# A two-layer attention and FFN kernel: attention sums from one pass of products, the output projection moved behind the second down product

## The reference

```python
x = x + autocorrelation(layernorm(x), ctx, ctx)      # FFT correlation, 8 best lags, weighted shifts
x = x + linear_with_8_adapters(layernorm(x))
x = x + grouped_attention(layernorm(x), ctx, ctx)    # 32 query heads, 8 key/value heads of 16
x = x + ffn(layernorm(x))                            # below
```

```python
h = relu(hidden @ up_w) ** 2
shared = h @ down_w
moe = (hidden @ fc1_w @ expert_w) * sum(top_2(hidden @ gate_w))
return layernorm(shared + moe @ fc2_w) * gamma + beta
```

## Time and profile before

| what | value |
|---|---|
| median of 3 runs | 685.81 us (684.9 to 689.61) |
| the profiled execution | 687.42 us |
| its span | 685.6 us |
| TensorE, share of the span | 95% |
| VectorE, ScalarE, GpSimd | 75%, 63%, 55% |
| granted clock of TensorE | 0.999 |

### The profile page before, as it was taken

How to read it: one execution, slowest core, us unless ns; L and a number is a source line. 1 busy time by engine, 2 the same in 40 slices (tenths; PEclk the granted TensorE clock), 3 DMA queues, 4 the chain that set the end, 5 groups by cost and what they waited for, 6 DMA issues and landing times.

```text
span 685.6 us, 12653 instructions
## 1 busy us (share of the span) xinstructions
PE 654.6 (95%) x3964; PEld 482.3 (70%) x3964; DVE 511.4 (75%) x1140; ACT 432.0 (63%) x793; POOL 378.5 (55%) x464
## 2 busy tenths in 40 slices
PE   7889999999999898999999999999999999998986
PEld 3455666666656476788778787887878878786775
DVE  4999998999975877777677677776777767775444
ACT  4788888888746785574655846658367474674221
POOL 1388999888775534435455354554454545535351
PEclk9999999999999999999999999999999999999999
DMA  8334434352126321121212312113021221211000
GB/s 269 121 109 124 139 123 124 123 180 98 62 94 173 117 79 33 46 64 61 63 35 57 90 33 61 45 49 90 31 61 54 69 61 31 61 31 47 17 16 31
DMA packets 32551, 54.37 MB, mean 79 GB/s; under 512 B 5344, under 2 KB 7136, under 8 KB 32512
## 3 DMA queue, kind: packets, MB, share of 16 engines
q1 hardware_dynamic: 32512, 53.90, 26.6%
HBM read 36.84 MB, written 8.39 MB: 66 GB/s over the span
## 4 chain that ended last, share of the span: by engine, by line
PE 78%; DVE 11%; issue 4%; DMA 3%; ACT 3%; POOL 1%; SPq 0%; POOLq 0%; DVEq 0%; ACTq 0%
PE ps_b L1295 8%; PE ps_b L1297 7%; PE ps_b L1296 7%; PE wide L1295 7%; PE wide L1297 6%; PE wide L1296 6%; PE ps_b L1496 4%; PE ps_a L1340 4%; PE bank L1432 3%; DMA ctx_t<-in_ctx 3%; PE wide L1422 3%; PE ps_b L1350 3%; PE ps_a L1295 2%; PE ps_a L1297 2%; PE wide L1550 2%
## 5 line engine op out<-in xcount | busy, mean ns | idle before, releaser
L780 POOL TENSOR_TENSOR va<-mv,small 128x1 f32<-128x1 f32 x80 | 15.3, 192 | 149.0 <-DVE mv L1274 79.5
L745 ACT ACTIVATE stage<-wide 128x512 f32<-128x512 f32 x30 | 16.3, 595 | 83.8 <-PE bank L1597 83.7
L868 POOL TENSOR_TENSOR y_l<-y,y_h 128x512 fp32r<-128x512 f32 x16 | 21.9, 1370 | 72.5 <-ACT y_h L653 72.5
L1142 DVE RECIPROCAL y<-ps_b 128x256 f32<-128x256 f32 x32 | 55.9, 1748 | 0.4 <-PE ps_b L1496 0.4
L676 ACT ACTIVATE probs<-wide 128x1024 f32<-128x1024 f32 x32 | 32.8, 1025 | 36.1 <-PE wide L1550 36.1
L1295 PE MATMUL wide<-up_h,t_h 128*128 128x512 f32 x128 | 52.1, 407 | 1.5 <-DVE t_l L1226 1.5
L1297 PE MATMUL wide<-up_h,t_l 128*128 128x512 f32 x128 | 50.9, 398 | 0.0
L1296 PE MATMUL wide<-up_l,t_h 128*128 128x512 f32 x128 | 50.4, 394 | 0.0
L1295 PE MATMUL ps_b<-down_h,ht_h 128*128 128x512 f32 x120 | 49.6, 413 | 0.4 <-DVE ht_l L1214 0.4
L782 POOL TENSOR_TENSOR rs<-va,small 128x1 f32<-128x1 f32 x80 | 44.5, 557 | 6.3
L1297 PE MATMUL ps_b<-down_h,ht_l 128*128 128x512 f32 x120 | 47.2, 393 | 0.0
(11 more groups left out here) (244 smaller groups left out, 2155.9 us busy)
## 6 DMA issues: line engine op xcount, KB each, us to landing
q_stack<-qt_h SPq DMA_DIRECT2D x128, 64.0 KB, 2.0
ctx_t<-in_ctx SPq DMA_DIRECT2D x16, 256.0 KB, 2.7
x_res<-in_x SPq DMA_DIRECT2D x16, 256.0 KB, 2.9
x_in<-x_rows SPq DMA_DIRECT2D x16, 256.0 KB, 2.7
ctx_t<-in_ctx_turned SPq DMA_DIRECT2D x16, 256.0 KB, 2.9
x_res<-x_rows SPq DMA_DIRECT2D x16, 256.0 KB, 2.9
out<-stage SPq DMA_DIRECT2D x15, 256.0 KB, 3.0
x_in<-in_x SPq DMA_DIRECT2D x8, 256.0 KB, 3.0
```

What stands on the lines that cost most here:

```text
L1142: dve.reciprocal(y[:, :, b, :], part[:, 1]).then_inc(S["den_s"], 1)
```

## The change

`attend` keeps its form for the tiles 0 and 1 (`apart(t)`). For the others `vbd` holds ones beside the values (set once, at tile 2), and a product takes 64 rows, one head of one batch, so that the numerators and the denominators of head h come out of one product, into bank 2 + h, on neighbouring groups of 16 partitions. ScalarE copies both banks into `sums` and writes the first head's numerators, masked by `place[0]`, into y (`attended_out`). Eight moves bring the denominators onto the numerators' partitions (`denominators`, 16 partitions of 2 KB each). VectorE adds the second head's numerators (`numerators`), takes the reciprocal in two instructions (`inverted`: 128 and 384 elements) and multiplies (`attended`).

The output projection goes behind `down(i, 1)`, its products with `y_l` come last, and the maxima's transposes stand ahead of these. `turned_hidden` and the down products come earlier; keys, queries and scores change places. On the other engines the calls follow. In the opening turn `down_low(0)` moves behind the reciprocals, `down_low(1)` into turn 0, and `down_high(1)` to the turn's end. The increments of `vf_s` and `dft_lo`, for which no engine waited, are dropped.

```diff
+            def denominators(t):
+                if live(t) and not apart(t):
+                    wait(sp, S["wo_ps"], t)
+                    for h in range(2):
+                        sp.wait_ge(S["sums_s"], 3 * (t - APART) + h + 1)
+                        for p in range(PAIRS):
+                            at, beside = STACK * p + HD * h, STACK * p + HD * (1 - h)
+                            sp.dma_start(den[at:at + HD], sums[h][beside:beside + HD]).then_inc(S["den_in"], 16)
...
             def body2(i):
                 load2(i + 4)
-                stacked(i + 3)
                 residual(i + 2)
+                denominators(i + 2)
                 t = i - 1
                 if live(t):
                     sp.wait_ge(S["o_s"], t + 1)
                     sp.dma_start(rows(out_rows, t), z_of(t)).then_inc(S["out_stored"], 16)
+                stacked(i + 3)
```

```diff
                 if opening(i):
-                    guard_rows(2)
-                    query_high(3)
-                    down_high(1)
+                    y_high(i + 2)
+                    queries_stacked(i + 3)
                 else:
-                    query_high(i + 4)
-                    guard_rows(i + 3)
+                    queries_stacked(i + 3)
+                    y_high(i + 2)
+                guard_rows(i + 3)
+                query_high(i + 4)
                 weights_of(i + 3, 0)
+                weights_of(i + 3, 1)
                 t = i + 1
                 if live(t):
                     act.wait_ge(S["rt_out_ps"], 2 * t + 2)
...
+                if opening(i):
+                    down_high(1)
                 if closing(i):
                     hidden_high(NT - 1, 1)
-                weights_of(i + 3, 1)
```

```diff
+            def attended_out(t):
+                if live(t) and not apart(t):
+                    act.wait_ge(S["pv_ps"], 2 * t + 2)
+                    act.wait_ge(S["qy_ps"], capped(1, t + 2))
+                    for h in range(2):
+                        act.activation(sums[h][:].rearrange("p g b q -> p b g q"),
+                                       bank[2 + h].rearrange("p (b g q) -> p b g q", b=2, g=GROUPS), ACT.Copy
+                                       ).then_inc(S["sums_s"], 1)
+                    wait(act, S["wo_ps"], t)
+                    act.activation(y[:].rearrange("p g b q -> p b g q"),
+                                   bank[2].rearrange("p (b g q) -> p b g q", b=2, g=GROUPS), ACT.Copy, scale=place[0]
+                                   ).then_inc(S["sums_s"], 1)
```

VectorE, functions and turn:

```diff
+                elif live(t):
+                    dve.wait_ge(S["sums_s"], 3 * (t - APART) + 3)
+                    dve.scalar_tensor_tensor(y[:], sums[1][:], place[1], y[:], ALU.mult, ALU.add).then_inc(S["den_s"], 1)
+
+            def inverted(t, groups):
+                if live(t) and not apart(t):
+                    dve.wait_ge(S["den_in"], DEN_MOVES * (t - APART + 1))
+                    dve.reciprocal(den[:, groups], den[:, groups]).then_inc(S["den_s"], 1)
+
+            def attended(t):
+                if live(t) and not apart(t):
+                    dve.wait_ge(S["den_s"], 2 * APART + 3 * (t - APART + 1))
+                    dve.tensor_tensor(y[:], y[:], den[:], ALU.mult).then_inc(S["y_s"], 1)
...
                 t = i
                 if live(t) and not final(t):
                     hidden_low(t, 0)
+                keys_low(i + 3)
+                queries_low(i + 3)
+                numerators(i + 2)
+                if isinstance(i, int) and i == 0:
+                    down_low(1)
+                context_low(i + 4)
+                maxima(i + 3, 0)
+                inverted(i + 2, slice(0, 1))
+                t = i
+                if live(t) and not final(t):
+                    hidden_low(t, 1)
+                inverted(i + 2, slice(1, GROUPS))
                 attended(i + 2)
+                maxima(i + 3, 1)
+                normalised(i + 4)
...
+                if opening(i):
+                    down_low(0)
                 values(i + 3)
+                third(i + 2)
+                norm_low(i + 4)
...
+                keys_biased(i + 4)
+                third_norm(i + 2)
                 queries(i + 4)
```

Between `normalised` and `down_low(0)` stand the maximum and the sum of the gate; between `norm_low` and `keys_biased` the sum z and its statistics. GpSimd does the square of the hidden rows ahead of `y_low`, and `y_low` follows it. TensorE:

```diff
+            def attend_ready(t):
                 if live(t):
                     pe.wait_ge(S["vbd_s"], t + 1)
                     wait(pe, S["kv_s"], capped(1, t + 2))
                     wait(pe, S["z_s"], t - 2)
+                    pe.wait_ge(S["probs_s"], 2 * t + 2)
...
+                elif live(t):
+                    for b in range(2):
+                        for p in range(PAIRS):
+                            for h in range(2):
+                                k = slice(SEQ * h, SEQ * (h + 1))
+                                last = pe.matmul(bank[2 + h][STACK * p:STACK * (p + 1), HALF * b:HALF * (b + 1)],
+                                                 vbd[k, b, p].rearrange("k h d -> k (h d)"), probs[k, b, p, :],
+                                                 start=True, stop=True)
                         last.then_inc(S["pv_ps"], 1)
...
+            def output(t, between):
+                if live(t):
+                    pe.wait_ge(S["y_hi"], t + 1)
+                    for g in range(GROUPS):
+                        pe.matmul(bank[2], cols(y_h, g, P), cols(wo_h, g, D), start=(g == 0), stop=False)
+                        pe.matmul(bank[2], cols(y_h, g, P), cols(wo_l, g, D), start=False, stop=False)
+                    between()
                     pe.wait_ge(S["y_lo"], t + 1)
                     for g in range(GROUPS):
+                        last = pe.matmul(bank[2], cols(y_l, g, P), cols(wo_h, g, D), start=False, stop=(g == GROUPS - 1))
                     last.then_inc(S["wo_ps"], 1)
```

More of the change, by code:

```diff
@@ L94, in constants @@
     small[:, ONES0:ONES0 + 2 * HD] = np.kron(np.eye(2), np.ones((SEQ, HD)))
+    small[:, PLACE0:PLACE0 + 2] = np.tile(np.repeat(np.eye(2), HD, axis=0), (PAIRS, 1))
     for p in range(PAIRS):
@@ L136, in build @@
         ones_bd = small[:, ONES0 - FIRST:ONES0 - FIRST + 2 * HD]
+        place = [small[:, PLACE0 - FIRST + h:PLACE0 - FIRST + h + 1] for h in range(2)]
         half, eps, minus = (small[:, c - FIRST:c - FIRST + 1] for c in (HALF0, EPS0, MINUS0))
@@ L157, in build @@
         x_in, ctx_t = sb("x_in", [P, D]), sb("ctx_t", [P, D])
+        with ExitStack() as tmp:
+            sums = [sb(f"sums{h}", [P, GROUPS, 2, SEQ], stack=tmp) for h in range(2)]
         x_h, x_l = sb("x_h", [P, D], F32R), sb("x_l", [P, D], F32R)
@@ L284, in build, with apart, folded @@
         LEAD2 = 4
+        APART = 2
+        def apart(t):
+            return isinstance(t, int) and t < APART
+        def folded(n, tiles):
+            return n * (min(max(tiles, 0), NT - APART) if isinstance(tiles, int) else tiles)
         MOVES = 16 * 2 * PAIRS
+        DEN_MOVES = 16 * 2 * PAIRS
         EARLY = NT - 2
@@ L1243, in body2 @@
                     dve.tensor_tensor(rw[:], lg[:, 0:1], lg[:, 1:2], ALU.add).then_inc(S["rw_s"], 1)
-                maxima(i + 3, 0)
-                context_low(i + 4)
-                if isinstance(i, int) and i < 0:
-                    third(i + 2)
-                    normalised(i + 4)
-                else:
-                    normalised(i + 4)
-                    third(i + 2)
-                maxima(i + 3, 1)
-                t = i
-                if live(t) and not final(t):
-                    hidden_low(t, 1)
                 if closing(i):
@@ L1594, in turned_hidden @@
                 if not final(t):
+                    wait(pe, S["ht_lo"], 2 * t + part)
                     wait(pe, S["qx_lo"], capped(1, t + 4))
@@ L1635, in body2 @@
                         last.then_inc(S["u_ps"], 1)
-                    routed_part(t, HALF, D + EXPERTS, bank[4])
-                rough_scores(i + 3, 0)
-                t = i
-                if live(t) and not final(t):
-                    wait(pe, S["y_s"], capped(2, t + 3))
-                    down(t, 0)
-                output(i + 2)
+                if not opening(i):
+                    rough_scores(i + 3, 0)
                 t = i
@@ L1662, in body2 @@
                     down(t, 1)
+                output(i + 2, lambda: turned_maxima(i + 3))
+                turned_norm(i + 4)
+                t = i + 1
+                if live(t):
+                    wait(pe, S["x3_s"], capped(1, t + 2))
+                    routed_part(t, 0, HALF, bank[2][:, HALF:])
                 if closing(i):
```

87 lines of the change are left out of this document (43 added, 44 removed).

## The result

The changed kernel takes 698.13 us (median of 4, 696.93 to 698.83) beside 685.75 us of the kernel before on the same chip: ratio 1.0165, 95% interval 1.014 to 1.0191, so slower by more than the 1% that a measurement tells. The profiled execution took 698.8 us, with a span of 697.0 (before: 687.42 and 685.6). The forecast was 694.

The account below looks back on a forecast made before the run. TensorE, busy 27.98 of 28.00 us in a steady turn, was taken as the bound. Opening +0.2, twelve steady turns +4.8, turn 12 +1.6, turn 13 +2.0, turn 14 -0.5 gave +8.1 on 685.8: 694 us, range 680 to 703.

Parts of the forecast that it names:

- The new attention block: TensorE's `attend`: two rounds of eight 64-row products instead of four rounds, 0.97 us instead of 1.86, saving 0.89 a turn.
- The evacuations and the denominators' transfers: ScalarE's three more copies per tile and the eight denominator DMAs issued by SyncE: both covered by idle time, cost nothing.
- The chain to the output: From `down(i, 0)`'s handover (D) through copy, subtraction, 384-element reciprocal and `y_h`: 5.44 us against 4.75 of TensorE work, waiting 0.69.
- Rival B: Reciprocal of 384 elements from SBUF takes under 1.86 us, so no wait for `y_h`: 683.5 us; chance 0.22.
- The wait for x3: TensorE ahead of the lower routed part, with only `turned_norm` to fill the time: 0.52 us a turn, 0.10 before.
- The changes of block: Three more TensorE blocks follow a block of another kind, at 0.06 us each: 0.18 us a turn.
- Rival C: Row halves in the attention block do not overlap when there are column strips too: 706.5 us; chance 0.08.
- Rival D: VectorE comes late to `third`, its norm waiting for GpSimd's `y_low`; the wait for x3 doubles: 701 us; chance 0.12.
- Steady turn: One turn of pass 2: 28.08 - 0.89 - 0.10 + 0.69 + 0.52 + 0.18 = 28.48 us, so +4.8 us for twelve.
- Guard rows first: ScalarE's `guard_rows` can run when the maxima are turned, well ahead of `scores`: no effect on time.
- The opening turn: Turn i = -1: x3 wait about 3 us, second weights 0.8, other waits of some 4 us go; about +0.2 us.
- Turn 13: Near the end: output handed over at 19.3 us, then `third`, statistics and norm before the next transposes; 23.5 against 21.5, +2.0.

Follow-up runs that it names:

- three groups first: Changed kernel with three groups of the inverses ahead of the hidden layer's second part and one behind, instead of one and three: 685.66 us, ratio 0.9995.
- order alone: Changed kernel's order of work with the old two-form attention products for every tile and the old reciprocals from PSUM: 698.12 us, ratio 1.0177.
- Four groups first: Changed kernel with all inverses ahead of the hidden layer's second part (`hidden_low`): first executions 689.52 to 696.36 us, repeat 691.08 us, ratio 1.007.
- query copy first: Changed kernel with ScalarE's copy of the turned tile ahead of the four guard rows, as in the kernel before: 711.92 us, ratio 1.0382.

## Why the prediction was right, and where it was off

The forecast (slower, 694 us) had the right sign and, in the steady turns, the right mechanism, with the measured 698.13 inside its range. The opening turn and turn 13 were off in mechanism too. By its steps:

- **The new attention block** at 0.97 us: 1.03. The eight 64-row products do run at once. By the Trainium skill (TensorE: Matmul & The Clock Gate, "Measured speedup vs the span model") packed tiles fall short of their number, which made an estimated 1.3 us of this block; the trace doesn't agree: it has 1.03.
- **The evacuations and the denominators' transfers** at nothing: right in the steady turns. In the whole run VectorE waited twice for those transfers (0.7 us in turn 12 and 4.7 in turn 13), and in no steady turn; TensorE's wait for `y_h` in turn 13 is 0.8 us, no longer than elsewhere.
- **The chain to the output**, 5.44 us after D: down(i, 0) hands over at 456.05 and the output starts at 461.54, so 5.49. The reciprocal of 384 elements took 2.54 us (2.55). The wait of 0.69 was 0.74, and three groups first took it away, for 0.84 a turn, since the first product behind a wait also takes 0.1 us longer. Rival B, a cheap inverse from SBUF, is out.
- **The wait for x3** at 0.52: 0.52. **The changes of block** at 0.18: order alone puts the whole order at 0.42 a turn in place of my 0.60, and 0.52 less the 0.10 of before makes up all of it, so the 0.18 does not show. Rival C is out by the block's length. Rival D is out too: `third` starts when the output ends, at 465.09, 0.20 us behind the handover at 464.89.
- **Steady turn** 28.48: 28.48. From the experiments its parts are -0.83 (form), +0.84 (chain) and +0.42 (order), where I had -0.89, +0.69 and +0.60: three misses of 0.06 to 0.18 us that cancel. That the sum is exact to 0.01 us is luck; that it is near is not.
- **Guard rows first, "Nothing"**: right as a difference to before, but for another reason than I gave. Had ScalarE kept its old order, the steady turn would have been 29.59.
- **The opening turn** at +0.2 us: this is the term that failed most. It took +2.5. My own figures (3 + 0.8 - 4) add up to -0.2, not +0.2. I had seen the wait for `x3` (3 us forecast; the lists of waits of this stretch have 0.5 before and 2.5 after) and the 0.8 us for the second weights. But the other waits that I set against them at 4 us were only 2.3 us in the list of the kernel before (maxima 1.5, norm 0.4, scores 0.4). They went, that for `y_l` grew from 0.5 to 1.1, and a new one of 0.4 came; and I had no term for the clock. In the five profiles that keep the wait and in which the clock stayed up, the turn is 26.3 to 26.8 us, so 1.3 to 1.8 us of it are the clock in those executions in which it falls. Four groups first, one kernel in two profiles, puts it at 28.25 - 26.76 = 1.5 us.
- **Turn 12** at +1.6: +1.7. **Turn 13** at +2.0: +3.4. The waits were as forecast. What was missing is the lower clock: in query copy first, with the same wait ahead of turn 13 and the clock at 1.00, that turn takes 23.41 us, the forecast +1.9. **Behind turn 14's start** at -0.5: -0.4.

The sum of +8.1 became +11.4 in the profiled executions: 2.3 and 1.4 us more at those two places, less the 0.7 by which turn -1 started sooner. So the failed step is this: my sum took the clock as constant and made each wait cost its own length. At these two places, in the executions in which the clock fell, it cost 1.5 us more, beside the waits misjudged in the opening turn.

## What to carry to other kernels

When an instruction that waits for another engine stands between two halves of a long piece of work, put into the first half as much as fits ahead of the moment at which the wait would end anyway: here moving 256 elements of a reciprocal across one waiting subtraction was worth 12 us of 698. A saving on the bounding engine (0.83 us a turn) is worth nothing while its result's chain is awaited for as long; look for it not in the busy times but in the first product behind the wait. And when an order is changed, go through every engine's list: of two neighbours on ScalarE, swapped, one order cost 1.1 us a turn.

## What the runs showed that I had not expected

**The clock falls around some waits, not all.** TensorE's 12 products of the lower routed part take 467.36 - 465.84 = 1.52 us in turn 6 and 267.89 - 265.16 = 2.73 us in turn -1 of the same trace, at a granted clock of 0.50:

```profile
265.16 0.58 PE L1364 MATMUL ps_b<-rt_h,t_h 128*128 128x256 f32 x1 [2.48 <-DVE x L1217]
...
267.89 0.77 PE L1636 MATMUL wide<-q_stack,k_stack 128*128 128x256 f32 x4
```

In turn -1, nine profiles of this study keep the wait of 2.0 to 2.5 us. In 4 of them the clock fell, between 0.4 us before the wait's end and 1.5 us behind it; it fell in none of the 4 in which the wait was filled or removed. That alone is weak: at 4 in 9, four profiles without a fall would come by chance about one time in ten. At the start of turn 13 it is stronger. The clock fell in 8 of the 10 profiles with the 1.94 us wait, in 5 of them before the wait had ended, and in none of the 3 with the other ending, which chance would give less than once in a hundred. There it stayed low for 3.4 us in half of the eight and for 6.8 us in the other half. So at turn 13 the wait is part of the cause; it isn't all that decides, since at turn -1 the same kernel showed both levels, and what else does stays open. In 7 of the 14 profiles the clock also fell once between 15 and 45 us of the span, in pass 1, which no experiment edits: part of the scatter between executions comes from there.

The Trainium skill (TensorE: Matmul & The Clock Gate, "HAM oscillation — how this bites in real kernels") tells of a kernel whose pauses for data let the clock fall, so that each next stretch starts cold. These traces agree with it in kind, though not every such wait did it here.

**A VectorE operation can last as long as the GpSimd operation beside it.** The sum for `rw`, one element per partition, takes 0.16 us in turn 6 and 1.02 us in turn -1, where it begins during GpSimd's `y_l` and ends as that does:

```profile
259.99 1.02 DVE L1322 TENSOR_TENSOR rw<-lg 128x1 f32<-128x1 f32 x1
...
463.24 0.16 DVE L1322 TENSOR_TENSOR rw<-lg 128x1 f32<-128x1 f32 x1
```

```profile
259.54 1.44 POOL L911 TENSOR_TENSOR y_l<-y,y_h 128x512 fp32r<-128x512 f32 x1
```

The norm ahead of it stretches in the same way: it takes 1.19 us in turn 6 of this trace and 1.46 in that of three groups first, beginning while `y_l` runs and ending 0.3 us behind it. In a steady turn of four groups first the order in time is the other one: the norm begins 0.28 us ahead of `y_l` and takes 0.53 us, and the sum for `rw`, which begins while `y_l` runs, takes 1.05. No run takes `y_l` away, so the cause is read from these coincidences and not tested. The sum was off the critical path in the steady turns, but in turn -1 it stood ahead of `down_low(0)` and `third`.
